# Turning every second x1 tile with 32x32 block transposes and sixteen small transfers instead of on TensorE

## What is computed

```
q, k = rot(x @ Wq) / 8, rot(x @ Wk)              # 4 heads of 64
v, g = x @ Wv, silu(x @ Wg)                      # 4 heads of 128
o = chunk_retention(q, k, v, gamma)              # a state per head, carried from chunk to chunk of 64
x1 = layernorm(x + (rmsnorm(o) * gn * g) @ Wo)
h = silu(x1 @ Wgate.T / 127) * (x1 @ Wup.T / 127)
out = layernorm(x1 + h @ Wdown.T / 127)
```

## Time and profile before

| | |
|---|---|
| time, three runs | 423.06, 423.6, 423.93 us; median 423.6 |
| the profiled execution | 423.2 us, its span 421.5 us |
| PE busy | 412.1 us, 98% of the span, 4698 matmuls |
| DVE, ACT, POOL busy | 313.2, 268.2, 183.2 us |
| TensorE clock granted | full (0.999) but for the last microseconds |
| a slot from 9 to 31 | 12.46 us |

### The profile page before, as it was taken

The page is one execution under the profiler, slowest core; times in us unless marked ns, Lnnn a source line. Parts: engine busy times, 40 slices in busy tenths (PEclk is TensorE's granted clock), DMA queues, the critical chain, the costliest instruction groups (busy, mean ns, idle before and its releaser), DMA issues.

```text
span 421.5 us, 12747 instructions
## 1 busy us (share of the span) xinstructions
PE 412.1 (98%) x4698; PEld 394.4 (94%) x4698; DVE 313.2 (74%) x912; ACT 268.2 (64%) x812; POOL 183.2 (43%) x330
## 2 busy tenths in 40 slices
PE   8999999998999999999999999999999999999994
PEld 6899999998999999999999999999999999998994
DVE  4999776677777777867777867777777777784975
ACT  6678655577666766766766766666666666654551
POOL 2532344355344455334355344445443434442654
PEclk9999999999999999999999999999999999999999
DMA  8931010101020201102020110201110010100001
GB/s 284 360 131 52 0 51 2 53 14 39 12 68 2 76 2 40 39 2 77 2 55 25 40 40 2 76 2 40 39 26 29 2 51 2 40 14 15 15 25 55
DMA packets 14352, 19.99 MB, mean 47 GB/s; under 512 B 1488, under 2 KB 9808, under 8 KB 14288
## 3 DMA queue, kind: packets, MB, share of 16 engines
q1 hardware_dynamic: 14144, 19.08, 14.1%
q10 hardware_dynamic: 144, 0.07, 0.1%
HBM read 14.94 MB, written 4.19 MB: 45 GB/s over the span
## 4 chain that ended last, share of the span: by engine, by line
PE 94%; DVE 2%; DMA 1%; issue 1%; POOL 1%; ACT 0%; SPq 0%; POOLq 0%; DVEq 0%; ACTq 0%
PE b_rows L527 30%; PE b_rows L545 20%; PE b_ffn L527 20%; PE b_turn L763 3%; PE b_head L793 3%; PE b_head L801 3%; PE b_turn L558 2%; PE b_state L820 2%; PE b_ffn L711 2%; PE b_head L722 2%; PE b_head L814 1%; PE b_rows L541 1%; DMA wf_int<-in_w_proj 1%; PE b_head L689 1%; PE b_head L685 1%
## 5 line engine op out<-in xcount | busy, mean ns | idle before, releaser
L2032 POOL TENSOR_TENSOR h_lo<-wf_int,h_hi 128x256 fp32r<-128x256 f32 x96 | 70.0, 742 | 121.7 <-ACT h_hi L1210 121.7
L527 PE MATMUL b_ffn<-x1T_hi,wf_hi 128*128 128x256 f32 x384 | 92.0, 279 | 0.1
L527 PE MATMUL b_ffn<-x1T_lo,wf_hi 128*128 128x256 f32 x384 | 91.5, 278 | 0.0
L1199 ACT ACTIVATE wf_int<-b_ffn 128x256 f32<-128x256 f32 x96 | 36.9, 384 | 59.5 <-PE b_ffn L527 59.4
L527 PEld LDWEIGHTS b_ffn<-x1T_hi,wf_hi 128*128 128x128 f32 x384 | 72.2, 188 | 0.6 <-DVE x1T_lo L1668 0.2
L527 PEld LDWEIGHTS b_ffn<-x1T_lo,wf_hi 128*128 128x128 f32 x384 | 72.2, 188 | 0.0
L545 PE MATMUL b_rows<-wp_hi,xT_hi 128*128 128x256 f32 x230 | 66.4, 289 | 1.2 <-issue 1.2
L545 PE MATMUL b_rows<-wp_hi,xT_lo 128*128 128x256 f32 x244 | 66.5, 277 | 0.0
L545 PE MATMUL b_rows<-wp_lo,xT_hi 128*128 128x256 f32 x230 | 63.8, 277 | 0.0
L1608 DVE TENSOR_TENSOR wf_int<-b_ffn,wf_int 128x256 f32<-128x256 f32 x96 | 40.2, 419 | 26.3 <-ACT wf_int L1199 25.7
L1186 ACT ACTIVATE sq<-b_head 128x128 f32<-128x128 f32 x120 | 33.3, 278 | 28.7 <-PE b_head L801 19.6
(11 more groups left out here) (191 smaller groups left out, 1166.5 us busy)
## 6 DMA issues: line engine op xcount, KB each, us to landing
xT_raw<-in_xT SPq DMA_DIRECT2D x16, 256.0 KB, 2.8
x_sb<-in_x SPq DMA_DIRECT2D x16, 256.0 KB, 3.0
out<-wf_int SPq DMA_DIRECT2D x30, 128.0 KB, 1.8
wf_int<-in_w_ffn SPq DMA_DIRECT2D x6, 384.0 KB, 6.7
wf_int<-in_w_proj SPq DMA_DIRECT2D x6, 256.0 KB, 4.7
rope_sb<-in_rope SPq DMA_DIRECT2D x4, 256.0 KB, 5.7
rope_q<-in_rope_by_row SPq DMA_DIRECT2D x2, 512.0 KB, 9.5
wo_raw<-in_w_o SPq DMA_DIRECT2D x1, 512.0 KB, 6.4
```

The source lines that it names most:

```text
L527: mm = pe.matmul(dst, a, b, start=(i == 0 and j == 0 and not begun), stop=(i == n - 1 and j == len(passes) - 1 and not more), skip_group_c ...
L1199: act.activation(act_g[:, u], b_ffn[u][:, 0:256], ACT.Silu, scale=SCALE).then_inc(silu_done[j], 1)
L2032: pool.tensor_tensor(h_lo[:, ring, hb], h_full[:, u], h_hi[:, ring, hb].bitcast(F32), ALU.subtract).then_inc(h_split[j], 1)
```

## The change

For the ten even tiles 8, 10, ..., 26 (`moved_x1`), `turn_x1` is left out. Instead:

- DVE, right after `norm_1`, runs `block_x1`: one 32x32 block transpose of the 128x256 tile into `x1_blocks` (each 32x32 block is turned in its place).
- SP, after the store of that (odd) slot, runs `move_x1`: sixteen transfers within SBUF, each of 32 partitions x 2 x 32 numbers (8 KB in runs of 128 B), which put block row i and column j to j and i, into `x1T_raw`.
- ACT and DVE split such a tile not at the head of slot n+4 but in its middle: on ACT after `split_h` 1 and ahead of `gate` 2, once all sixteen transfers have landed (`x1_moved`); on DVE after the rotation's cosines and ahead of `stats_2`. They read `x1T_raw` in SBUF in place of a PSUM bank.
- The wait for `next_kept`, which `turn_x1` made for the bank, now stands ahead of the first FFN block of a slot; the FFN's wait for `x1T_split` counts one tile less where the even tile is not split yet.

```diff
+        x1_blocks = wf_int[:, 5 * 512 + 256:6 * 512].bitcast(F32)
+        x1T_raw = wf_int[:, 6 * 512:6 * 512 + 256].bitcast(F32).rearrange("p (k n) -> p k n", k=KD)
...
+        def moved_x1(n):
+            return n % 2 == 0 and CHUNKED <= n < NT - 5
...
+            def move_x1(n):
+                blocks = x1_blocks.rearrange("p (k j c) -> p k j c", k=KD, c=BLOCK)
+                sp.wait_ge(x1_blocked, (n - CHUNKED) // 2 + 1)
+                sp.wait_ge(x1T_split, n - 1)
+                for i in range(P // BLOCK):
+                    src = slice(i * BLOCK, (i + 1) * BLOCK)
+                    for j in range(P // BLOCK):
+                        sp.dma_start(x1T_raw[j * BLOCK:(j + 1) * BLOCK, :, src], blocks[src, :, j, :]).then_inc(x1_moved, 16)
...
             for s in range(NT):
                 slot(s, s // TS, s % TS)
+                if s >= PACKED and moved_x1(s - 3):
+                    move_x1(s - 3)
...
-                if exists(n):
+                if exists(n) and not moved_x1(n):
                     pe.wait_ge(x1_ready, n + 1)
...
+                    behind = 3 if moved_x1(s - 3) else behind
                     pe.wait_ge(x1T_split, s - behind)
...
+                elif j == 0 and s < NT and t > 0:
+                    pe.wait_ge(next_kept, nexts_to(s - 1))
...
-                    act.wait_ge(x1T_done, n + 1)
+                    if moved_x1(n):
+                        act.wait_ge(x1_moved, x1_moves(n))
+                    else:
+                        act.wait_ge(x1T_done, x1_turns(n) + 1)
...
                 split_h(b, tb, 0)
                 split_h(b, tb, 1)
+                if moved_x1(s - 4):
+                    split_x1T(*at(s - 4, X1T_LAG))
                 gate(b, tb, 2)
...
+            def block_x1(n):
+                if n > CHUNKED:
+                    dve.wait_ge(x1_moved, x1_moves(n - 2))
+                dve.wait_ge(x1_ready, n + 1)
+                dve.transpose(x1_blocks, x1_of(n)).then_inc(x1_blocked, 1)
...
                 norm_1(*at(s - 3, X1T_LAG))
+                if moved_x1(s - 3):
+                    block_x1(s - 3)
                 sum_k(s, q, t)
```

More of the change, by code:

```diff
@@ L57 @@
 CHUNKED = PACKED - 1
+BLOCK = 32
 def rope_tables():
@@ L229, in build_block @@
         qkT_done, qkT_kept = sem("qkT_done"), sem("qkT_kept")
+        x1_blocked, x1_moved = sem("x1_blocked"), sem("x1_moved")
         v_copied, g_gated = sem("v_copied"), sem("g_gated")
@@ L315, in ffn_before, with x1_moves, x1_turns @@
             return (b, 0) if j == 2 else (b - 1, j + 1)
+        def moved_x1(n):
+            return n % 2 == 0 and CHUNKED <= n < NT - 5
+        def x1_moves(n):
+            return 16 * (P // BLOCK) ** 2 * ((n - CHUNKED) // 2 + 1)
+        def x1_turns(n):
+            return sum(not moved_x1(i) for i in range(n))
         def packed_rows(s, k):
@@ L1143, in split_x1T @@
                     ring, at = ((t - 3) // 2) % 2, ((t - 3) % 2) * P
-                    act.wait_ge(x1T_done, n + 1)
+                    if moved_x1(n):
+                        act.wait_ge(x1_moved, x1_moves(n))
+                    else:
+                        act.wait_ge(x1T_done, x1_turns(n) + 1)
                     if exists(n - 4):
                         act.wait_ge(ffn_done[2], n - 2 if (t - 3) % 2 == 0 else n - 3)
-                    act.copy(x1T_hi[:, ring, :, at:at + P],
-                             x1_bank(s, t)[:, 0:KD * P].rearrange("p (k n) -> p k n", k=KD)).then_inc(x1T_high, 1)
+                    src = x1T_raw if moved_x1(n) else x1_bank(s, t)[:, 0:KD * P].rearrange("p (k n) -> p k n", k=KD)
+                    act.copy(x1T_hi[:, ring, :, at:at + P], src).then_inc(x1T_high, 1)
             def gate_v(s, q, t):
@@ L1266, in packed_slot @@
                 else:
-                    split_x1T(*at(s - 4, X1T_LAG))
+                    if not moved_x1(s - 4):
+                        split_x1T(*at(s - 4, X1T_LAG))
                     gate_v(*at(s, -1))
@@ L1618, in norm_1 @@
                         dve.wait_ge(z2_ready, n - 7)
-                        dve.wait_ge(x1T_done, n - 7)
+                        if not moved_x1(n - 8):
+                            dve.wait_ge(x1T_done, x1_turns(n - 8) + 1)
                     dve.tensor_scalar(x1_of(n), z1[:], mv1[:, 0:1], rs1[:, 0:1], ALU.subtract,
                                       ALU.mult).then_inc(x1_ready, 1)
+            def block_x1(n):
[3 more added lines that the diff above has]
+                dve.transpose(x1_blocks, x1_of(n)).then_inc(x1_blocked, 1)
             def norm_2(s, q, t):
@@ L1667, in split_x1T @@
                     dve.wait_ge(x1T_high, n + 1)
-                    dve.tensor_tensor(x1T_lo[:, ring, :, at:at + P],
-                                      x1_bank(s, t)[:, 0:KD * P].rearrange("p (k n) -> p k n", k=KD),
+                    src = x1T_raw if moved_x1(n) else x1_bank(s, t)[:, 0:KD * P].rearrange("p (k n) -> p k n", k=KD)
+                    dve.tensor_tensor(x1T_lo[:, ring, :, at:at + P], src,
                                       x1T_hi[:, ring, :, at:at + P].bitcast(F32), ALU.subtract).then_inc(x1T_split, 1)
@@ L1812, in packed_slot @@
                 b, tb = s - 1, (s - 1) % TS
-                if s > PACKED:
+                if s > PACKED and not moved_x1(s - 4):
                     split_x1T(*at(s - 4, X1T_LAG))
```

## The result

The changed kernel takes 480.35 us (median of four runs, 475.75 to 482.0) against 423.76 for the kernel before (four runs). The ratio is 1.132, 95% interval 1.124 to 1.140: 57 us slower. The prediction had the direction and not the size (+4 us), and its range ended at 433. The profiled execution took 479.26 us; its span is 477.4 us, 55.9 more than before.

The account below looks back on a forecast made before the run. PE was taken as the bound; per tile a 0.2 us wait plus 0.5 for fetches less 0.21 saved, taken as +0.4, gave +4 us over ten tiles: 427.6 us, range 421.2 to 433, the forecast's own 424.5 to 430.5.

Parts of the forecast that it names:

- The clock: PE's granted clock behind a wait: the prediction has no term for it.
- the sum: Per tile 0.2 us wait plus 0.5 for fetches less 0.21, taken as +0.4; ten tiles +4 us, 427.6.
- What bounds the kernel, and the saving: PE is busy throughout slots 17 and 18; leaving out two x1 transposes saves 0.21 us per tile, 2.1 in all.
- On DVE: Block transpose behind `norm_1` takes 0.43 us, upper end 0.54; `turn_qk` has 0.7 us of room, so nothing is paid.
- The pace of issues: SP's sixteen issues in a row follow at 0.47 us each, bounds 0.40 and 0.52.
- a cost for a pattern: Three-dimensional pattern on both sides issues at 0.52 us or lands after 2 us: 431 to 436, rival's chance 14%.
- The landing: From a small transfer's issue on SP to its landing: 1.4 us, taken between 0.7 and 1.7.
- the store's row: Profile row of a 128 KB store landing in 1.7 us, set against the skill's fixed 2.0 us per transfer.
- The disturbance by instruction fetches: Fetches sharing the DMA engines stretch SP's issues or the landing: 0.5 us per tile on average.
- The point where PE waits: Last landing after 212.6 in slot 18 delays `turn_q`, then PE's v projection, one for one.
- the sample slot: Slot 18, where tile 14, the sample for all ten tiles, must have its transfers landed.
- The xT load: Load behind the sixteen issues on SP lands at 214.7, needed by ACT at 219.73: 5 us of room, nothing paid.

Follow-up runs that it names:

- the last run: Late-split kernel, nine tiles' sixteen transfers given other ends in HBM or SBUF; ran once, not used for times; issues 0.42 to 0.43 or 0.60 us.
- the shapes: Late-split kernel with other shapes of the sixteen transfers in seven of ten tiles; ran once, not used for times; issues 0.59 to 0.62 us.
- the filling: Changed kernel plus sixteen 128x128 matmuls with unread results on PE ahead of the even slots' v projection: 466.93 us, ratio 1.099.

## Why the prediction was wrong

The step that failed is the time from the block transpose to the last landing: the pace of the issues above all, and the landing with it. The clock, which the sum held at nothing without a reason, made the loss half as large again. The steps in turn:

- **What bounds the kernel, and the saving**: right. 0.21 us per tile, 2.1 in all; the kernel without transfers gave 2.3.
- **On DVE**: right. The block transpose took 0.445 us (0.43 taken), ended 0.02 to 0.04 ahead of SP's first issue, and `turn_qk` waited for nothing.
- **The pace of issues, "I take 0.47, bounds 0.40 and 0.52"**: this step failed. It was 0.64 from start to start, outside the bounds. My row was six loads from HBM, and for such loads 0.47 holds (7.1 us for fifteen starts of tile 8 in the last run); there was no row of a transfer within SBUF. The upper bound of 0.52 came from imagining a cost for a pattern, which the shapes showed to be none. 15 x 0.17 makes 2.6 us per tile, all of it past the point where PE waits.
- **The landing**: 1.8 us, not 1.4; 8 KB within SBUF take as long as the 128 KB store (1.7). My reading of the store's row had subtracted a data time that isn't there to subtract. The 2.0 us of the Trainium skill (DMA: Bandwidth & Descriptors, Anatomy of one DMA) were nearer, though that section gives them for DMAs that GpSimd issues, and these are SP's.
- **The disturbance by instruction fetches**: right in kind, a little small. The ten rows of sixteen issues take 10.2 us undisturbed and 10.2 to 11.2 in the trace, 0.5 more on average. In seven rows one issue took 1.14 to 1.64 us, and each time with a large fetch (queue q8, 1.0 to 1.3 us long) under way. In two others the fetch began only after the start of the last issue, whose landing took 2.7 and 3.0 us. Together that is some 0.7 us per tile, where 0.5 were counted.
- **The point where PE waits**: right to 0.1 us. 8.2 us behind the block transpose were allowed; in the sample slot the landing came at 12.0 and PE waited 3.81.
- **The xT load**: right, nobody missed it, with 3 us less of room than I counted.
- **The clock**: left out of the sum altogether. Behind waits of 3.3 to 4.4 us it cost another 1.7 to 2.6 us per tile, 19 of the 57 us. For the 0.7 us that I had expected nothing would have been lost by it: in the kernel with twelve transfers it didn't fall behind gaps of 0.65 to 1.65 us. My range had no case in which it mattered.

With the measured pace and landing, the forecast's own sum is 0.2 + 2.6 + 0.4 + 0.6 (fetches and rounding) less 0.21, 3.6 us per tile, 36 in all, and 19 for the clock: 55 of 56. The structure held; a price at a sharp edge was guessed from the wrong kind of row, and the edge was not seen as one: behind it each 0.1 us of pace costs 1.5 us a tile, and the clock on top.

## What to carry to other kernels

Before a step is handed to a row of small transfers, count their issues: here 0.64 us for each within SBUF, and it is the last one that the reader waits for; fewer, larger transfers (five through HBM landed in half the time of sixteen within SBUF) or half a slot more of room turned the same idea from 13% slower to 0.5 to 0.7% faster. When TensorE is the bound, a new wait can cost more than itself: ten of about 4 us cost half as much again in granted clock, ten of 1.3 us on average a quarter. And where a forecast stands on an edge, price the far side of the edge too, with a bound from an operation of the same kind or with an honest gap where there is none.

## What the runs showed of the hardware

- SP's issues in a row: 0.60 us (median of 160, 0.64 from start to start) within SBUF, whatever the shape from 4 to 32 KB, and from HBM to HBM; 0.42 to 0.43 between HBM and SBUF in five of six cases (0.46 to 0.47 from start to start). The same xT load was issued in 0.43 us behind a row of the cheap kind and in 0.58 to 0.60 behind one of the dear kind.
- 8 KB within SBUF land 1.8 us after the start of their issue, the same as 32 KB (1.8, and 1.9 for 128x2x32).
- In seven of the changed kernel's ten rows of sixteen, one issue stretched to 1.1 to 1.6 us, each time with a large instruction fetch (1.0 to 1.3 us) under way.
- VectorE's 32x32 block transpose of 128x256 f32 takes 0.445 us, about as long as other operations on the tile (0.39 to 0.54).
- TensorE's granted clock fell to half behind each of ten gaps of 3.3 to 4.4 us: in seven slots after PE had started again, for 3.4 us, in three within the gap, for 6.8. With twelve transfers it fell behind gaps of 2.35 and 2.42 us, with the gap filled behind an idle rest of 2.29, and not behind eight of 0.65 to 1.65. With the filling the mean granted clock rose from 0.951 to 0.995 and the kernel took 13.4 us less.
